# A depthwise 3x3 neighbour sum as eight accumulating matmuls with diagonal matrices, instead of sixteen VectorE steps a group

## What is computed

```python
# z = layer norm over channels of x, x2 = z * z
Pk = per group of 8 channels: x2 @ gamma_k            # an 8x8 channel mix
k = gamma_s[..., 0] * mask                            # 3x3 per channel, the centre is 0
Ps = depthwise 3x3 convolution of x2 with k, "SAME"   # 8 neighbours, a factor for each channel and place
norm_pool = 1 / sqrt(Pk + Ps + (beta + 1e-6))
x = x + z * norm_pool * gamma_outside + beta_outside
```

## Time and profile before

| what | value |
|---|---|
| time, median of 3 runs | 723.12 us |
| lowest and highest run | 722.76 and 730.02 us |
| span of the profiled execution, first to last instruction | 721.9 us |
| TensorE, VectorE busy | 540.6 us, 523.5 us |
| ScalarE, GpSimd busy | 377.9 us, 283.2 us |
| mean granted TensorE clock | 0.932 |

### The profile page before, as it was taken

The page is one execution under the profiler, slowest core; times in us unless marked ns, Lnnn a source line. Parts: engine busy times, 40 slices in busy tenths (PEclk is TensorE's granted clock), DMA queues, the critical chain, the costliest instruction groups (busy, mean ns, idle before and its releaser), DMA issues.

```text
span 721.9 us, 8643 instructions
## 1 busy us (share of the span) xinstructions
PE 540.6 (75%) x3010; PEld 214.2 (30%) x3010; DVE 523.5 (73%) x926; ACT 377.9 (52%) x440; POOL 283.2 (39%) x240
## 2 busy tenths in 40 slices
PE   2314674589777988799778978798879786975776
PEld 1213223232323332343224323333333221321312
DVE  3266367868798979887998898889978796466312
ACT  2112712566566656756575657555766464543532
POOL 2122156034534453536362544365245433334013
PEclk9999975699999999999999999999999998998699
DMA  4500600063106230605041503350145005500240
GB/s 67 96 9 1 133 0 0 7 128 87 32 1 134 50 69 15 133 12 108 16 107 27 119 16 72 62 119 16 38 81 117 17 14 106 118 16 0 48 86 15
DMA packets 27834, 41.39 MB, mean 57 GB/s; under 512 B 11792, under 2 KB 19088, under 8 KB 27792
## 3 DMA queue, kind: packets, MB, share of 16 engines
q1 hardware_dynamic: 27152, 38.75, 26.2%
q0 software_dynamic: 640, 2.10, 1.0%
HBM read 38.22 MB, written 2.62 MB: 57 GB/s over the span
## 4 chain that ended last, share of the span: by engine, by line
DVE 39%; DMA 22%; PE 15%; issue 8%; POOL 7%; SPq 5%; ACT 4%; POOLq 0%; DVEq 0%; ACTq 0%
DMA WB<-w_scratch 18%; DVE nacc L1132 6%; PE yP L859 5%; PE hP L844 4%; SPq L402 3%; DMA w_scratch<-wTs 3%; DVE YW L1179 2%; POOL stat_c L486 2%; PE sA L760 2%; DVE xsplit L969 2%; PE sA L770 2%; DVE xcen_b L962 2%; POOL stat_b L486 2%; DVE xnrm L962 1%; DVE xnrm L957 1%
## 5 line engine op out<-in xcount | busy, mean ns | idle before, releaser
L691 ACT ACTIVATE H<-hP,b 128x1024 f32<-128x1024 f32 x192 | 209.2, 1110 | 82.6 <-PE hP L844 81.5
L859 PE MATMUL yP<-H,w 128*64 128x512 f32 x768 | 211.3, 632 | 21.3 <-DVE ACC L1179 19.3
L844 PE MATMUL hP<-xT,w 128*128 128x512 f16 x768 | 209.9, 399 | 4.3 <-ACT H L691 4.3
L556 POOL TENSOR_TENSOR ACC<-ACC,YW 128x512 f32<-128x512 f32 x96 | 125.6, 1313 | 194.6 <-DVE YW L1179 194.5
L844 PEld LDWEIGHTS hP<-xT,w 128*128 128x128 f16 x768 | 65.9, 101 | 145.8 <-issue 84.5
L1179 DVE SCALAR_TENSOR_TENSOR YW<-yP,b,WB 128x512 f32<-128x512 f32 x96 | 71.3, 744 | 34.2 <-PE yP L859 34.2
L859 PEld LDWEIGHTS yP<-H,w 128*64 128x64 f32 x768 | 40.1, 138 | 103.3 <-issue 89.0
L1132 DVE SCALAR_TENSOR_TENSOR nacc<-PAD,taps,nacc 128x256 f32<-128x256 f32 x112 | 60.5, 540 | 3.7
L1179 DVE SCALAR_TENSOR_TENSOR ACC<-yP,b,WB 128x512 f32<-128x512 f32 x32 | 23.1, 746 | 46.9 <-DMA WB<-w_scratch 46.9
L540 POOL TENSOR_SCALAR nrg<-nacc,go_col 128x512 f32<-128x512 f32 x8 | 12.6, 1574 | 68.9 <-ACT nacc L659 68.9
L584 ACT ACTIVATE xsq<-xcen 128x512 f32<-128x512 f32 x24 | 15.0, 626 | 36.1 <-DVE xcen L941 36.0
(11 more groups left out here) (144 smaller groups left out, 761.9 us busy)
## 6 DMA issues: line engine op xcount, KB each, us to landing
WB<-w_scratch SPq DMA_DIRECT2D x32, 1024.0 KB, 9.9
X<-in_x SPq DMA_DIRECT2D x8, 256.0 KB, 12.0
out<-X POOLq DMA_DIRECT2D x8, 256.0 KB, 2.8
H<-in_L_ffn_W SPq DMA_DIRECT2D x2, 512.0 KB, 6.2
H<-in_L_ffn_W SPq DMA_DIRECT2D x2, 256.0 KB, 4.2
w<-in_L_ffn_W SPq DMA_DIRECT2D x1, 512.0 KB, 4.8
w_scratch<-wTs SPq DMA_DIRECT2D x16, 32.0 KB, 1.8
w<-in_L_ffn_W SPq DMA_DIRECT2D x1, 256.0 KB, 4.1
```

What stands on the lines that cost most here:

```text
L556: pool.tensor_tensor(ACC[l][:, cols], ACC[l][:, cols], YW[:, u % 4, :], ALU.add).then_inc(summed, 1)
L691: nc.scalar.activation(H[:, s % RING, :], hP[s % 2][:, :], ACT.Gelu, bias=b1[l][:, e * ch + c:e * ch + c + 1], scale=1.0 / WS)\
L844: mm = nc.tensor.matmul(hP[s % 2][:, hf * HALF:(hf + 1) * HALF], w1[l][:, sp, w, :], xT[l][g % 2][:, hf * HALF:(hf + 1) * HALF], start=(sp ...
L859: mm = nc.tensor.matmul(yP[hf][a * C:(a + 1) * C, :], w2[l][:, (2 * j + a) * ch + c, :], H[:, (2 * ch * j + 2 * c + a) % RING, hf * HALF:( ...
```

## The change

The eight neighbours are added on TensorE, in the same PSUM bank and right behind the channel mix. For each neighbour there is a diagonal 128x128 matrix `tap_mats[:, n, :]` with the factors of the channels, and the moving operand is the shifted window of `PAD`. All 512 columns go in one matmul, so there are eight more f32 matmuls a group. The sixteen VectorE steps are gone. ScalarE takes the logarithm straight from `sC`; `nlog`, `nrs` and `nrg` are one buffer. The matrices are made once by eight VectorE steps in `prepare("experts1")`, from `ident32` and the column of `taps`.

```diff
-    cd=dict(centre_c=1, sums_c=1, norm_c=3, pool0=5, pool1=6, pool2=7, pool3=7, turn_u=10, centre_d=10,
+    cd=dict(centre_c=1, sums_c=1, norm_c=3, turn_u=10, centre_d=10,
...
-        nacc = sb("nacc", [P, 2, SIDE, SIDE])
-        nlog = nrs = nacc
-        nrg = sb("nrg", [P, 2, SIDE, SIDE])
+        nlog = nrs = nrg = sb("nlog", [P, 2, SIDE, SIDE])
+        tap_mats = sb("tap_mats", [P, 8, P])
...
-            count, k = {"turn_c": (sqT, 2), "pool": (tap, 9), "turn_u": (cz, 1), "turn_d": (trS["d"], 1),
+            count, k = {"turn_c": (sqT, 2), "pool": (nact, 1), "turn_u": (cz, 1), "turn_d": (trS["d"], 1),
...
                 elif k == "norms":
-                    act.wait_ge(tap.sem, tap.at(g))
+                    act.wait_ge(cmm.sem, cmm.at(g))
                     exp_ln_tables()
-                    nc.scalar.activation(nlog[:, :, :, :], nacc[:, :, :, :], ACT.Ln, bias=nbias[:, 0:1])\
-                        .then_inc(nact.sem, 1)
+                    if g >= 1:
+                        act.wait_ge(utr.sem, utr.at(g - 1))
+                    nc.scalar.activation(nlog[:, :, :, :], sC[:, :].rearrange("p (q r c) -> p q r c", q=2, r=SIDE),
+                                         ACT.Ln, bias=nbias[:, 0:1]).then_inc(nact.sem, 1)
...
                 elif k == "pool0":
                     pe.wait_ge(*c_read("pool", g))
                     pe.wait_ge(sqT.sem, sqT.at(g))
-                    nc.tensor.matmul(sC[:, :].rearrange("p (q r c) -> p q r c", q=2, r=SIDE), mix[:, :],
-                                     PAD[:, :, 1:SIDE + 1, 1:SIDE + 1], start=True, stop=True).then_inc(cmm.sem, 1)
+                    if g == 0:
+                        pe.wait_ge(prep, PREP["experts1"])
+                    sums = sC[:, :].rearrange("p (q r c) -> p q r c", q=2, r=SIDE)
+                    nc.tensor.matmul(sums, mix[:, :], PAD[:, :, 1:SIDE + 1, 1:SIDE + 1], start=True, stop=False)
+                    for n, (i, j) in enumerate(NEIGHBOURS):
+                        mm = nc.tensor.matmul(sums, tap_mats[:, n, :], PAD[:, :, i:i + SIDE, j:j + SIDE],
+                                              start=False, stop=(n == 7))
+                    mm.then_inc(cmm.sem, 1)
...
                     did(v.tensor_scalar(nbias[:, :], nbias[:, :], 1e-6, None, ALU.add))
+                    for n, (i, j) in enumerate(NEIGHBOURS):
+                        did(v.tensor_scalar(tap_mats[:, n, :], ident32[:, :], taps[:, 3 * i + j:3 * i + j + 1], None,
+                                            ALU.mult))
...
-                elif k in ("pool0", "pool1", "pool2", "pool3"):
...
-                    for n in range(4 * part, 4 * part + 4):
...
-                        v.scalar_tensor_tensor(out=nacc[:, q], in0=PAD[:, q, i:i + SIDE, j:j + SIDE],
-                                               scalar=taps[:, 3 * i + j:3 * i + j + 1], in1=base, op0=ALU.mult,
-                                               op1=ALU.add).then_inc(tap.sem, 1)
```

More of the change, by code:

```diff
@@ L54 @@
 LAG = 4
+NEIGHBOURS = [(i, j) for i in range(3) for j in range(3) if (i, j) != (1, 1)]
 NO_FINAL = (-1, -1, -1, -1)
@@ L123 @@
 LOADS = {"in": 4, "out": 4, "experts0": 9, "conv1": 7, "experts1": 7}
-PREP = {"in": 3, "out": 7, "bias": 8, "experts0": 12, "experts1": 17}
+PREP = {"in": 3, "out": 7, "bias": 8, "experts0": 12, "experts1": 25}
 def build_metaformer(nc, x, W_in, dt_bias, A_log, D_param, ln_gamma, ln_beta, W_out, g0_w, g0_b, m0_W1, m0_b1,
@@ L284, in build_metaformer @@
         cmm = count("cmm", 1)
-        tap = count("tap", 18 - 2)
         nact = count("nact", 2)
@@ L930, in prepare @@
                     dve.wait_ge(loaded["conv1"], 16 * LOADS["conv1"])
+                    dve.wait_ge(ident_made, 4)
                     did(v.tensor_scalar(nbias[:, :], nbias[:, :], 1e-6, None, ALU.add))
+                    for n, (i, j) in enumerate(NEIGHBOURS):
+                        did(v.tensor_scalar(tap_mats[:, n, :], ident32[:, :], taps[:, 3 * i + j:3 * i + j + 1], None,
+                                            ALU.mult))
                 assert steps[0] == PREP[which]
```

## The result

The changed kernel takes 760.71 us, median of 4 runs (759.42 to 763.03), against 722.94 us: a ratio of 1.0491 with a 95% interval of 1.0456 to 1.0525. It is 38 us slower; 765 was forecast, in a range of 757 to 777. The profiled execution has a span of 759.9 us, 38.0 more than before.

A forecast was written before the change was run, and what follows sets the result against it. TensorE's and VectorE's queues, meeting almost together at the gate, were taken to bound the kernel. Terms 25.5 + 4.8 + 7.4 + 2.1 + 2.0 = 41.8 us on the 721.9 span give 763.7, with 1.2 around it 765 us; range 757 to 777.

The forecast's parts named there:

- The two queues at the gate: At the first gate step (line 980), TensorE's and VectorE's work arrive almost together, VectorE 0.7 us behind TensorE.
- The price of a matmul: Sixteen added TensorE instructions a group at 0.46 us each, 7.4 us, with weight loads hidden beneath the running instruction.
- The rival with open loads: Weight loads on TensorE lie exposed: 10.4 us a group for the added matmuls, 789 us in all; chance 0.07.
- the one of cheaper passes: The added TensorE passes cost only 4.4 us a group, so the time is about 742 us; chance 0.05.
- The rate of 131 ns: Skill page's figure per 512-column matmul on TensorE: the sixteen would take 2.1 us, the time staying near 727.
- The gate: In a middle group line 980 starts 5.1 us later, at 290.1 instead of 285.0, behind TensorE's delayed gate product.
- I find nothing that gives it back: Behind line 980, top2 to turn_d are one chain; the 3.00 and 1.05 us TensorE waits move along, giving nothing back.
- The clock: In the first group TensorE's clock is still rising: the sixteen instructions take 9.2 us, line 980 comes 2.1 later.
- start to the first channel mix: Eight added VectorE preparation steps of about 0.25 us ahead of the first gate, covered by nothing: 2.0 us.
- second to sixth group: Five groups each lengthened by the 5.1 us later gate step: 25.5 us.
- seventh: Group whose wait for xsplit_b is 1.94 us: of 7.4 us of matmuls, 4.8 remain after absorption.
- eighth, to the end: Last group, without a next mixer: TensorE's slots are back to back, so the full 7.4 us counts.

The follow-up runs named there:

- both works: Changed kernel with the sixteen VectorE steps put back in their old slots, their result unread: 764.29 us, ratio 1.0535.
- the two-slot move: Steps behind the sum (gate, top2, send, norms to turn_d) two slots earlier: kernel before 696.47 us, changed kernel 712.45, with half-precision neighbours 670.49.

## Why the prediction was right, point by point

**What bounds it.** The two queues at the gate, with TensorE 0.7 us ahead, held in the middle groups: without the matmuls the gate gained 0.6, with half of them it lost 1.1, with both works it stood where the change put it. The step from there to the period was looser: the gate is 4.7 us later in the undisturbed middle groups, and their periods grew by 3.9 to 5.2.

**The price of a matmul.** 0.46 us an instruction was taken, 0.429 measured at the upper level (6.86 us, not 7.4). The rate was read off a pair, and the pair takes 0.95 us in the changed kernel too (359.30 to 360.25); the sixteen behind it run closer. The weight loads lie beneath, as taken: those of line 815 keep the length of the earlier trace rows and the block has no gap. The rival with open loads falls, and so does the one of cheaper passes. The rate of 131 ns from the Trainium skill, page "TensorE: Matmul & The Clock Gate", section "Back-to-back issue gap", is not reached here in half precision either: the eight f16 instructions are 0.22 us apart. The section itself names no precision for that rate.

**The gate.** 5.1 us later was forecast, 4.6 to 4.7 measured, the difference being the block's length.

**What comes behind it.** "I find nothing that gives it back" was a little wrong. `send` came 384.37 - 359.30 = 25.07 us behind the mix, 21.05 before: 4.0 later and not 4.6. The gate steps account for it. The one at line 1019 took 1.33 us from 288.74 while GpSimd added up (line 556, 288.72 to 289.99) and takes 0.22 at its new time, and `wgt` takes 1.15 instead of 0.27, again beside that addition (line 555 now):

```profile
288.74 1.33 DVE L1019 TENSOR_TENSOR gt<-gt 128x64 f32<-128x64 f32 x1
```
```profile
382.32 0.22 DVE L1030 TENSOR_TENSOR gt<-gt 128x64 f32<-128x64 f32 x1
...
383.07 1.15 DVE L1037 TENSOR_TENSOR wgt<-gt,gs 128x64 f32<-128x64 f32 x1
```

The waits at `turn_d` and `Vs` stayed, as said, and the mean period of the middle groups, 80.0 us, is near the 80.4 named.

**The clock** was a term that the forecast had for the first group alone. In two of the five middle groups the block fell on a lower granted clock (0.81 in the row shown above), and the distance to the gate was 21.25 instead of 19.56, 1.7 us each:

```profile
278.28 1.45 PE L813 MATMUL sC<-PAD,mix 128*128 128x512 f32 x2 [0.90 <-ACT PAD L648]
```
```profile
299.53 0.23 DVE L991 SCALAR_TENSOR_TENSOR gt<-sA,gb 128x64 f32<-128x64 f32 x1 [4.06 <-PE sA L716]
```

**The sum,** by the starts of the channel mix in both traces:

| part | forecast | measured |
|---|---|---|
| start to the first channel mix | 2.0 | 126.11 - 123.08 = 3.0 |
| first group | 2.1 | 71.80 - 71.66 = 0.1 |
| second to sixth group | 25.5 | (597.81 - 197.91) - (570.19 - 194.74) = 24.5 |
| seventh | 4.8 | 75.15 - 71.71 = 3.4 |
| eighth, to the end | 7.4 | (759.9 - 672.96) - (721.9 - 641.90) = 6.9 |
| all | 41.8 | 38.0 |

The middle groups are right in part by luck, two errors that cancel: the pass and the gate steps were cheaper, the clock dearer. The three undisturbed periods grew by 4.4 us in the mean, the two with the slow block by 5.6; forecast was 5.1 for each. The seventh group grew by 3.4 and not 4.8; half a microsecond of that is the shorter block, the rest stays open.

In the first group the block took 127.95 to 136.90, 8.95 us, where 9.2 was forecast, and line 991 came 3.1 us later behind the mix, where 2.1 was forecast. The second experts' gate step was still 2.1 us later there, the next channel mix only 0.1. Between them lies a difference in the granted clock that no term of the forecast covers: in the 18 us from 29 us behind the mix it read 0.81 before and 1.00 after. That the clock gave the 2 us back fits, but no run separates it:

```profile
152.10:170.10 18.00, 15.99 (x84) 6.98 (x85) 12.27 (x27) 7.83 (x10) 5.02 (x4) 0.81 0.18 35
```
```profile
155.10:173.10 18.00, 12.90 (x90) 6.31 (x91) 14.08 (x32) 10.11 (x11) 4.20 (x4) 1.00 0.33 64
```

The start differs between executions by as much as its term: with the same preparation and the old order the first channel mix comes at 124.5 to 126.2 us in the profiles of these runs. So the 2.0 is borne out by the times of the kernel with the preparation alone, and not by this row.

## What to carry over

Two queues that meet at one step have to be timed to that step, not added up: what an engine saves is worth only its lateness there (0.6 us of 8.5 in the old order, 2.9 in the moved one), and what another engine takes on is free only up to its own slack (2.3 us), then it counts in full. And where an order is written out by hand, try the order by itself first: the two-slot move gave 28 us with the sum left on VectorE (724 to 696), 48 with the f32 matmuls (761 to 712) and 50 with the f16 ones (720 to 670). Moving the sum to TensorE paid only with both, cheap matmuls and the moved order: the cheap ones alone gave 0.5%, and the f32 ones lost 16 us even in the moved order.

## What the runs showed of the hardware that was not expected

- The granted clock can fall in the middle of a busy kernel. TensorE was busy 4.00 of 6 us just ahead of the block, while it waited for `xnrm` and `PAD`; the clock then read 0.81 over the next 6 us, and the block took 8.3 instead of 6.9. What set it off is not shown: in the group shown first TensorE was busy 4.01 of 6 us ahead of the block, with the same two waits, and the clock stayed at 1.00 over it. The kernel before isn't free of such falls either: just behind its waits at 304.00 and 305.66 the clock reads 0.72, and this is what the 0.98 of its period holds.

```profile
353.30:359.30 6.00, 4.01 (x48) 1.89 (x45) 5.57 (x8) 3.55 (x5) 4.05 (x3) 1.00 0.00 0
```
```profile
304.00:310.00 6.00, 4.95 (x30) 2.94 (x32) 4.14 (x6) 2.64 (x4) 0.00 (x0) 0.72 0.34 66
```

- A VectorE step of 128x64 took 1.33 us beside GpSimd's addition (line 556) and 0.22 without it. Not every GpSimd step does this: beside the scaling (line 539 of the changed kernel, 381.24 to 382.84) the same step, now line 1030, took 0.22 at 382.32.
